# First stage of a two-layer block: squared ReLU split on ScalarE and VectorE, the mean of squares as a column, and a first chunk of its own

## The reference

```python
xn = _layernorm(x)
h = _rms_norm(xn, norm_w)
gate = gelu(h @ fc_gate_w.T + fc_gate_b);  hs = h @ fc_w.T + fc_b
r = sigmoid(h @ fc_r_w.T + fc_r_b);        i = sigmoid(h @ fc_i_w.T + fc_i_b)
a = exp(-8 * softplus(alpha) * r);         s = sqrt(1 - a*a) * hs * i
out[t] = a[t] * out[t-1] + s[t]            # scan over a sequence
hs2 = out * gate + xn
h2 = _rms_norm(hs2, norm2_w)               # hs2 / sqrt(mean(hs2*hs2) + eps) * w
attn = (h2 @ mlp_fc_w.T + b) * gelu(h2 @ mlp_gate_w.T + b) @ out_w.T + out_b + hs2

hf = _bitlinear(xn, w_fc) + gate_s * (xn @ v.T @ fast_b.T @ u.T)
f = maximum(hf, 0) ** 2                    # squared ReLU, 1024 wide
ffn = _bitlinear(f, w_proj)                # ternary weights times a scale
x = x + attn + ffn
```

## Time and profile before

| | before |
|---|---|
| median of 3 runs | 2524.01 us |
| profiled execution, its own time | 2523.25 us |
| its span, first to last instruction | 2521.4 us |
| mean granted TensorE clock (1 is 2.4 GHz) | 0.905 |
| PE busy | 2101.1 us, 83% |
| DVE busy | 1938.3 us, 77% |
| ACT busy | 1403.8 us, 56% |
| POOL busy | 1306.0 us, 52% |

### The profile page before, as it was taken

One profiled execution on the slowest core, in us unless ns is written; L12 is line 12 of the kernel. 1 busy time (PEld: TensorE's weight loads), 2 busy tenths in 40 slices (PEclk: granted clock), 3 DMA queues, 4 the chain that ended last, 5 costly groups with the idle time before them and its releaser, 6 DMA issues. The chain is left out here.

```text
span 2521.4 us, 38434 instructions
## 1 busy us (share of the span) xinstructions
PE 2101.1 (83%) x12252; PEld 1684.0 (67%) x12252; DVE 1938.3 (77%) x2446; ACT 1403.8 (56%) x2490; POOL 1306.0 (52%) x945
## 2 busy tenths in 40 slices
PE   6888888888766778787888878766699999999995
PEld 5666676667542546455555555555599999999995
DVE  6566546654641899999999999999488888888883
ACT  5234323432415576767766676754377766666662
POOL 0432243224402788979797979796023334343442
PEclk9999999999877789898989889867799999999998
DMA  9011101110122223132223232223366676666663
GB/s 282 18 34 42 42 8 33 42 42 8 34 69 90 86 76 122 70 111 78 101 90 110 80 118 86 89 84 126 126 230 222 206 235 195 229 198 228 217 207 94
DMA packets 109259, 287.24 MB, mean 114 GB/s; under 512 B 20742, under 2 KB 85654, under 8 KB 90294
## 3 DMA queue, kind: packets, MB, share of 16 engines
q1 hardware_dynamic: 94870, 267.45, 30.5%
q0 software_dynamic: 14304, 18.75, 3.9%
HBM read 239.54 MB, written 50.82 MB: 115 GB/s over the span
## 5 line engine op out<-in xcount | busy, mean ns | idle before, releaser
L1270 POOL TENSOR_TENSOR m_work<-m_ux,m_bb 128x1024 f32<-128x1024 f32 x256 | 600.1, 2360 | 72.6 <-DVE m_hh L1579 66.2
L1427 ACT ACTIVATE m_da<-m_dl,m_A 128x512 f32<-128x512 f32 (+1 forms) x512 | 332.1, 681 | 196.4 <-DVE m_hh L1579 195.0
L2020 PE MATMUL e_h<-e_xTh,e_w1h 128*128 128x256 f32 x1248 | 353.8, 283 | 7.2 <-DVE e_xTl L1956 5.3
L2020 PE MATMUL e_h<-e_xTl,e_w1h 128*128 128x256 f32 x1248 | 349.8, 280 | 0.0
L2020 PE MATMUL e_h<-e_xTh,e_w1l 128*128 128x256 f32 x1248 | 349.7, 280 | 0.0
L1589 DVE TENSOR_TENSOR m_work<-m_hh,m_cb 128x1024 f32<-128x1024 f32 x256 | 312.7, 1222 | 38.5 <-PE m_cb L1670 17.1
L1699 PEld LDWEIGHTS m_y<-m_ident,m_work 128*128 128x128 f32 x2048 | 287.9, 161 | 57.3 <-issue 40.4
L1699 PE MATMUL m_y<-m_ident,m_work 128*128 128x128 f32 x2048 | 321.2, 309 | 1.2 <-DVE m_work L1589 1.2
L1579 DVE TENSOR_TENSOR_SCAN m_hh<-m_da,m_carry,m_work 128x1024 f32<-128x1024 f32 x128 | 300.0, 2344 | 6.3 <-ACT m_work L1438 6.3
L1579 DVE TENSOR_TENSOR_SCAN m_hh<-m_da,m_work 128x1024 f32<-128x1024 f32 x128 | 292.2, 2283 | 11.1 <-POOL m_work L1270 6.2
L1916 ACT ACTIVATE e_sg<-e_h,e_b 128x256 f32<-128x256 f32 x312 | 145.9, 468 | 202.0 <-PE e_h L2020 201.9
(11 more groups left out here) (296 smaller groups left out, 5080.6 us busy)
## 6 DMA issues: line engine op xcount, KB each, us to landing
m_bb<-scratch_bT SPq DMA_DIRECT2D x64, 1024.0 KB, 4.9
m_first<-in_w SPq DMA_DIRECT2D x20, 2048.0 KB, 8.5
e_w<-in_w SPq DMA_DIRECT2D x19, 2048.0 KB, 8.3
m_first<-in_w SPq DMA_DIRECT2D x20, 1024.0 KB, 10.9
e_w<-in_w SPq DMA_DIRECT2D x19, 1024.0 KB, 10.9
scratch_rec<-empty SPq DMA_DIRECT2D x39, 260.0 KB, 7.8
e_xg<-scratch_rec SPq DMA_DIRECT2D x39, 260.0 KB, 2.8
e_b<-in_b SPq DMA_DIRECT2D x39, 128.0 KB, 3.1
```

The lines of the kernel that those rows point to most:

```text
L1270: pool.tensor_tensor(bx[:, u % NB], ux[:, cols], slot.to_broadcast([P, HALF, T]), ALU.mult).then_inc(s_bx, 1)
L1427: act.activation(da[u % NA][:, i, i:T], dl[q % 2][:, e, i:T], ACT.Exp, scale=A[:, at:at + 1]).then_inc(s_exp, 1)
L2020: last = mm(hbank[m % HR][:, j], w[i][:, k, cols], x[i][:, k], start=(p == 0 and k == 0 and j == 0), stop=(p == 2 and k == KD - 1 and j == 1),
```

## The change

- `fTl` leaves POOL. ACT writes the square of the ReLU back into `relu_f[m]` in full precision, and later, after each of the first four gelus of the MLP, copies two of them into `fTh` (`high_f`). DVE subtracts two of them after each of its first four MLP products.
- `centre` of the next chunk moves from between the MF products to behind them: the first part ahead of O0, the others one by one behind O0, O1 and O2.
- MS turns round: `sq` becomes the weight and one column of `inv_d` the moving operand, eight matmuls of one column, so that the mean square of 128 tokens is a column. Square root and reciprocal are of 128x4 elements. A new product RB, ahead of F6, spreads the result over a 128x512 tile of PSUM, from which DVE reads it. PSUM places move with it (`LAST`).
- `row_scales` becomes three instructions, with both powers in one of 128x8.
- The preparation loads the vector and the two large weights first, does the low parts in other order, takes the row means as columns from `half_f` inside `project`, and makes the last matrices (`mean_j`, `means_j`) inside chunk 0, which PE and ACT now write apart as DVE did.

```diff
-FMS = 4
+FMS, FRB = 4, 6
+LAST = {"N0": 3, "N1": 6, "Q0": 5, "Q1": 4, "L": 7}
...
-        b = 5 if g == "L" else p % BANKS
+        b = LAST.get(g, p % BANKS)
...
             sp_.dma_start(xt[:], rows(dram["x"], 0)).then_inc(x_in, 16)
+            sp_.dma_start(vec[:], dram["vec0"]).then_inc(vec_in, 16)
+            sp_.dma_start(w_f, dram["w_f"]).then_inc(wf_in, 16)
+            sp_.dma_start(w_p, dram["w_p"]).then_inc(wp_in, 16)
             for dst, src in small_loads:
                 sp_.dma_start(dst, src).then_inc(small_in, 16)
-            sp_.dma_start(w_f, dram["w_f"]).then_inc(wf_in, 16)
-            sp_.dma_start(w_p, dram["w_p"]).then_inc(wp_in, 16)
...
                 pool.tensor_tensor(sm[:, 0], var, eps_ln[:], ALU.add).then_inc(done, 1)
-                pool.wait_ge(done, base + 1)
-                pool.tensor_tensor(sm[:, 1], sm[:, 0], neghalf[:], ALU.pow).then_inc(done, 1)
+                pool.tensor_scalar(sm[:, 1], var, 1.0 + eps_rms, eps_rms * EPS_LN, ALU.mult, ALU.add).then_inc(done, 1)
                 pool.wait_ge(done, base + 2)
...
+                pool.tensor_tensor(sm[:, 2:4], sm[:, 0:2], neghalf[:], ALU.pow).then_inc(done, 1)
...
-                for m in range(KH):
-                    pool.wait_ge(s_fh, c * KH + (m + 1))
-                    pool.tensor_tensor(relu_f[m], relu_f[m], relu_f[m], ALU.mult).then_inc(s_fsq, 1)
-                    pool.wait_ge(s_fsq, c * KH + (m + 1))
-                    pool.tensor_tensor(fTl[:, m], relu_f[m], f32(fTh[:, m]), ALU.subtract).then_inc(s_fl, 1)
...
-                    act.activation(fTh[:, m], relu_f[m], ACT.Square).then_inc(s_fh, 1)
+                    act.activation(relu_f[m], relu_f[m], ACT.Square).then_inc(s_fsq, 1)
+
+            def high_f(ms, c):
+                for m in ms:
+                    act.wait_ge(s_fsq, c * KH + (m + 1))
+                    act.activation(fTh[:, m], relu_f[m], ACT.Copy).then_inc(s_fh, 1)
...
                 wait_filled(act, "MS", c)
-                act.wait_ge(s_rinv, c + 1)
-                inc_drained(act.activation(rms, ps("MS")[:], ACT.Sqrt, bias=eps0[:, 0:1]), "MS")
+                inc_drained(act.activation(rms[:], ps("MS")[:, 0:SUB], ACT.Sqrt, bias=eps0[:, 0:1]), "MS")
+                if first:
+                    act.activation(sign_j, sign_j, ACT.Sign).then_inc(s_prepa, 1)
...
                     inc_drained(act.activation(mg[:, m % 2], ps(g)[:], ACT.Gelu,
                                                bias=vec[:, V0["mg_b"] + m:V0["mg_b"] + m + 1]), g)
+                    high_f(range(2 * m, min(2 * m + 2, KH)), c)
...
                 if first:
+                    means_j()
                     low_gates()
                 wait_drained(dve, "MS", c)
-                dve.reciprocal(rinv[:], rms).then_inc(s_rinv, 1)
-                dve.wait_ge(s_rinv, c + 2)
...
+                dve.reciprocal(rinv[:], rms[:]).then_inc(s_rinv, 1)
+
+                wait_filled(dve, "RB", c)
+                for k in range(KD):
+                    dve.tensor_tensor(h2h[:, k], hs2[:, k], ps("RB")[:], ALU.mult).then_inc(s_h2h, 1)
...
-                    if more and m >= KM - SUB:
-                        centre(xt, mv, small, s_ln, xn, hn, [m - (KM - SUB)])
+                    for j in range(2 * m, min(2 * m + 2, KH)):
+                        dve.wait_ge(s_fh, c * KH + (j + 1))
+                        dve.tensor_tensor(fTl[:, j], relu_f[j], f32(fTh[:, j]), ALU.subtract).then_inc(s_fl, 1)
+                if more:
+                    dve.wait_ge(s_st, c * 9 + 18)
+                    dve.wait_ge(s_pw, c * 3 + 6)
+                    centre(xt, mv, small, s_ln, xn, hn, [0])
...
+                    if more and s + 1 < SUB:
+                        centre(xt, mv, small, s_ln, xn, hn, [s + 1])
...
-            for m in range(KH):
-                at = m % (KH // 2) * P
-                for k in range(KD):
-                    last = mm(bank[3][:, m:m + 1], abs_f[:, k, m // (KH // 2), at:at + P], inv_d[:, 0:1], start=(k == 0),
-                              stop=(k == KD - 1))
...
+                        if prep and (name, m) == ("R", 1):
+                            pe.wait_ge(s_prepd, PREPD["z_l"] + 2)
...
                 for m in range(KH):
+                    if head and m == 0:
+                        pe.wait_ge(s_prepd, PREPD["u_s"] + 1)
+                    if head and m == FMS:
+                        mean_j()
                     if m == FMS:
                         wait_bank(pe, "MS", c)
-                        for k in range(KD):
-                            pe.wait_ge(s_sq, c * KD + (k + 1))
-                            last = mm(ps("MS")[:], inv_d[:], sq[:, k], start=(k == 0), stop=(k == KD - 1))
+                        pe.wait_ge(s_sq, c * KD + KD)
+                        for s in range(SUB):
+                            for k in range(KD):
+                                last = mm(ps("MS")[:, s:s + 1], sq[:, k, s * P:(s + 1) * P], inv_d[:, 0:1], start=(k == 0),
+                                          stop=(k == KD - 1))
                         inc_filled(last, "MS")
+                    if m == FRB:
+                        wait_bank(pe, "RB", c)
+                        pe.wait_ge(s_rinv, c + 1)
+                        pe.wait_ge(s_prepd, PREPD["scale_j"] + 1)
+                        for s in range(SUB):
+                            last = mm(ps("RB")[:, s * P:(s + 1) * P], rinv[:, s:s + 1].to_broadcast([P, P]), ident[:], start=True,
+                                      stop=True)
+                        inc_filled(last, "RB")
...
-            with pe.Fori(0, NCH - 1) as c:
-                chunk(c, True)
+            chunk(0, True, True)
+            with pe.Fori(0, NCH - 2) as c:
+                chunk(c + 1, True)
             chunk(NCH - 1, False)
```

250 lines of the change are left out of this document (130 added, 120 removed).

## The result

The changed kernel takes 2463.23 us, the median of 4 runs (2460.79 to 2468.20), against 2524.77 us for the kernel before in 4 runs beside them: a ratio of 0.9757, 95% interval 0.9746 to 0.9769, so 61.5 us or 2.4% less. The forecast was 2447 us with a range of 2436 to 2462. The direction was right, the gain too large by 16 us, and the median lies 1.2 us above the range. The profiled execution is the longest of the four, 2468.2 us of its own time, with a span of 2466.5 us.

A forecast was written before the change was run, and what follows sets the result against it. PE was taken to set the first stage's chunks, with its waits, 40.9 us on POOL's `fTl`, as what counts. Terms -67.6 - 11.8 + 9.1 - 1.6 - 4.5 = -76.4 us from 2523.25 gave 2446.9, forecast 2447 us, range 2436 to 2462.

The forecast's parts named there:

- Part 1: `fTl` on DVE and ACT: O0 falls to O1's length in chunks 0 to 6, -67.6 us.
- Part 3: MS and RB: RB's wait replaces the removed reciprocal, +1.3 us for each of chunks 1 to 7, +9.1 together.
- Part 2: Chunk 7 from F0 to O0: with POOL empty it takes chunk 6's time, -11.8 us.
- longer low clock: Rival at MS to RB: idle and one-column matmuls keep PE at half clock, +9.8 us, 2457 us; chance 20%.
- Part 4: POOL's scales: three instructions instead of seven, -1.6 us behind chunk 7.
- Part 5: Preparation and chunk 0: earlier weights and moved means, less new waits, -4.5 us.
- late `fTl`: Rival at O0: DVE or ACT is late, half of O0's excess stays, +34 us, 2481 us; chance 6%.
- the slower case: Rival over whole chunks: PE's clock does not hold, +96 us at 24 us more low clock, 2543 us; chance 2%.
- Preparation worse: Rival in the preparation: new waits add 5 to 8 us instead of taking 4.5, 2458 us; chance 9%.

The follow-up runs named there:

- x_poolf: The changed kernel with squares and subtractions for `fTl` back on POOL and `centre` between the products again: 2519.13 us, ratio 1.0000.
- b_dvef: The kernel before with only `fTl` moved to ACT and DVE and `centre` behind the products: 2442.92 us, ratio 0.9693.
- x_mswide: The changed kernel with the mean of squares as before the change (matmuls of 512 columns, no RB): 2447.44 us, ratio 0.9722.
- x_wide_t: The changed kernel with the old 512-column mean of squares, no RB, and POOL's residual addition in chunk 7 waiting for the squares: 2447.83 us, ratio 0.9711.
- x_tail: The changed kernel, with POOL's addition of the residual bias in chunk 7 waiting until the squares for MS are done: 2452.83 us, ratio 0.9751.
- the execution shown: The profiled execution of the changed kernel from the result's four runs, nothing further changed: 2468.2 us.
- the other two: Profiled executions of the changed kernel, unchanged, in the second and third groups of experiments: medians of the runs there 2460.37 and 2464.30 us.

## Why the prediction was right or wrong

**Part 1** (-67.6) was right. O0 takes 4.94 to 4.95 us in place of the forecast 4.9 and has no wait; x_poolf, without this part, is as slow as before, and b_dvef, with it alone, brings 78.1 us in the stage against 79.4 forecast for part 1 and chunk 7. A small loss was not in the sum: each O takes 0.08 us more than before the change, 0.3 a chunk. It is there in every kernel with the one-column MS and RB, also with the 128-column MS, and not in b_dvef, x_mswide and x_wide_t, so it belongs to part 3. In O1 of chunk 3 the products with `w_j` start 120 ns apart instead of 113. These kernels also have two small tiles (`rms`, `rinv`) allocated ahead of `fTh` and `fTl`, which the others lack; whether their place in memory or RB is the cause is open.

**Part 2** (-11.8) was too large by 2.5 to 4.1 us. Chunk 7 from F0 to O0 took 39.34 to 40.9 us, where part 2 and part 3's term gave 36.8. The step that failed is "with POOL empty I expect chunk 6's time": POOL was not empty. The residual's addition, which I had placed in the MLP, where DVE has slack, fell on the chain to the squares as soon as its transfer had landed, and held DVE for 2.13 us; x_tail took 1.9 us of it away and came to 37.45.

**Part 3** (+1.3 for each of chunks 1 to 7) is the term that put the execution shown out. There, from F0 to O0 a steady chunk lost 2.8 us (35.46 before, the mean of chunks 1 to 6, against 38.30), which is the "longer low clock" that stood among the rivals with 20% and as part 3's upper bound of 2.7. In the other two it lost 1.0 us, near the forecast, and MG0 left its wait 20.7 us behind F0 against 20.0 before, the 0.6 to 0.7 us that had been worked out. I had decided for the lower end because "the rows speak" for it, namely MS of before, which had run in a stretch of 0.79 too; but those rows were of a wide product. The mechanism was right (the reciprocal that is removed gains nothing, DVE waits for RB instead), the order of events too; the price of one-column products through the clock was taken from a stretch that had none. (The 3.0 us for MS "with before's mixture of clocks" does not follow either: 1.8 us at 0.79 are 2.3. MS took 3.4 us in the execution shown, 2.0 in the other.)

That part 3 is a loss, three kernels with the old form show: x_mswide and x_wide_t take 75.1 us a chunk, b_dvef 74.7, against 76.3 to 78.2. What the clock costs is about half of the low time from MS on, 4.6 to 9.1 us in the changed kernel and 2.3 in x_mswide and x_wide_t; what falls on F0 to F3 costs nothing, since DVE sets MS. By this estimate the changed kernel's chunk would be 73.6 to 74.0 us at full clock. The old form did run so: four chunks of x_mswide and x_wide_t with a clock of 1.00 from there on took 74.1 us each. At full clock the new form is thus neither worse nor better, and the clock makes the difference.

**Part 4** (-1.6) is right in kind: POOL's scales take 2.2 us instead of 3.4, and PE's stall behind chunk 7 fell from 9.65 to 8.36 us, by 1.3.

**Part 5** (-4.5): O0 of chunk 0 starts at 80.0, 81.1 and 83.1 us in the three executions, against 84.32, so -4.3, -3.2 and -1.2. The first is the forecast; the spread is larger than I allowed by naming one number.

**The sum.** Of the 21.5 us by which the execution shown missed, 11.4 are in chunks 1 to 6 (9.2 between F0 and O0, the low clock, and about 2 the slower O), 3.1 chunk 7, 0.6 chunk 0, and 6.5 the rest of the program. In the other two the first item is 0.1 or less, and the misses are 8.7 and 14.8 us: 1.6 and 3.6 ahead of chunk 1, 2.6 and 3.0 in chunk 7 and behind it, 4.5 and 8.0 in the rest. So three steps failed. Part 3 took the clock of one-column products near its lower end, +1.3 for 2.8 measured, in one execution of three. Part 2 expected chunk 6's time in chunk 7, 2.6 to 3.1 us too little in all three. And the whole rest of the program stood in the sum at nothing, because "the change touches nothing there"; it grew by 4.5 to 8.0 us. POOL's pause goes with about 4 us of that, the difference between the means of the traces with and without it (1789.3 and 1785.0); the remainder lies within what traces of either kind differ by. How the 16 us of the median divide is not known, since of the four runs of the result only the longest was traced.

**The range** reached 2462 with the longer low clock at 2457 inside it; what it had no room for was that case together with a lost part of chunk 7 and a rest of the program that grows. The bounds of the unknown parts, simply added, give 2434 to 2466, which would have held the median; the range that was written is narrower than its own terms. (And 2446.9 and 0.8 us are 2447.7, not 2447.)

**The rivals**: late `fTl` is excluded (no wait, x_poolf and b_dvef), the slower case too (0.93 to 0.95 over a whole chunk). Preparation worse did not happen.

## What to carry to other kernels

When a wide product is replaced by narrow ones, price the clock of what follows them too: behind a wait of 4.4 us, one-column matmuls had a stretch of 6.8 to 10.2 us at half speed around them, and a wide form that computes the same values 128 times over was faster. A part of a change that is hidden while another engine is late (x_poolf: nothing) can cost once that engine is relieved (the whole change against b_dvef beside it: 6 us in the first stage, 17 in the medians), so each part is to be priced in the kernel as it will be. And place the work that PE has in hand ahead of its wait: two more F ahead of MS, with a wide MS and POOL's late addition, took 37 us off the changed kernel, 24 of them in the first stage. Last, code that a change doesn't touch is not for that reason worth nothing in the sum: here it grew by 4.5 to 8.0 us, and one wait more on POOL in chunk 7 ended a pause of POOL in the second layer.
